# Counting a graph's edges on one core: ten blocks of 125 by 125 in a tile instead of five of 125 by 250, with the edge columns kept in two copies so that TensorE reads at fixed addresses

## The chip, the cores and the metric

The kernel runs as one program on one core of a Trainium2 chip. The time is the device time of one execution in microseconds. Before the change three runs took 710.77, 713.29 and 714.03 us; their median, 713.29 us, is the number that the changed kernel is set against.

## What is computed

A graph of 1250 nodes with 21250 edges, sorted by destination, goes through two graph-attention layers (eight heads of 128, then one of 768) and a feed-forward part with routed class tokens; each part starts with a layer norm and adds to its input. The attention of the reference is a softmax over the edges of each destination:

```python
e = jax.nn.leaky_relu(a_src[src] + a_dst[dst], NEG_SLOPE)
m = jax.ops.segment_max(e, dst, num_segments=n)
ex = jnp.exp(e - m[dst])
denom = jax.ops.segment_sum(ex, dst, num_segments=n)
alpha = ex / (denom[dst] + EPS)
out = jax.ops.segment_sum(alpha[:, :, None] * h[src], dst, num_segments=n)
```

The kernel makes the attention dense. It counts how often each pair (destination, source) occurs, takes the logarithm of the counts, and adds it to a 1250 by 1250 table of logits. What the change touches is how these counts are made.

## The kernel before

**Stages.** The first stage (0 to about 153 us) does three things side by side: it normalizes x and multiplies it by W1 in three parts (high by high, high by low, low by high; `products`, line L1336), it counts the edges (`count_edges` on TensorE, `one_hots` on VectorE), and it forms the attention vectors' products. Then come the eight heads (to about 405 us), the second layer's features, its attention, and the feed-forward part. The order on each engine is written out by hand.

**Counting.** The nodes are cut into NT = 10 tiles of NP = 125 destinations. A count matrix of one tile is 125 x 1250 and is stored as 125 rows by 1250 columns of another meaning: block w of SUB = 5 holds 25 destinations, its 125 rows are pairs (destination, group of 250 sources), and its GW = 250 columns are the source within its group. The edges lie in 170 chunks of CE = 125, one edge per partition. For a chunk and a block, VectorE compares the chunk's row number with an iota (`hotk`, 125 values) and its column number with an iota (`hotr`, 250 values); TensorE multiplies the two one-hot matrices, and so adds every edge of the chunk to the count in PSUM.

**Visits.** Since the edges are sorted, a block's edges lie in few neighbouring chunks. A small plan, made on VectorE from the first and last chunk of each block, gives each tile a first chunk (`start`), each block an offset (`away`), and the number of trips of a loop; with this input it is one trip for each of the ten tiles. A visit takes VISIT = 5 chunks. Chunks are kept in pairs for VectorE's sake, so `one_hots` builds TRIP = 3 pairs, six chunks, starting at an even one, and TensorE uses five of them: four at fixed places and a fifth that is the first or the last of the six, by the parity of the start. That fifth matmul reads at an address computed in registers (`end_of`, L1253); the four others are at L1251. L1242 and L1256 are small matmuls that open and close the sums.

**Who waits for whom.** Block w's one-hots are one buffer: VectorE waits for `hot_used[w]` before it writes it, TensorE for `hot_ready[w]` before it reads it. When a tile's counts are complete, ScalarE takes the logarithm, VectorE mends it (`mend`, L1949), and SyncE stores it and loads it back in the right shape. On VectorE the work between the one-hots of two tiles stands in this order: the next tile's row numbers (`local_rows`, L1913), the next tile's plan words loaded into registers (`plan_of`, L1917 and L1918), then `rows_of`, `column_scaled`, `rows_lower` (L1987) and `mend`. After tile 0 the attention vectors (`attz`, L2030), the low parts of W1 (L2038) and `wrow` (L2042) come instead. TensorE needs `attz` for L1387, `wrow` for L1393, and `rows_out` of tile t - 2 for `turn(t)` (L1266).

Of the kernel before, what the change touches and what calls it, by code (L numbers as in the profile page):

```python
# [41 lines left out]
SUB = 5  # L42
NW = NT * SUB
WD = N // NW
TRIP = 3
VISIT = 2 * TRIP - 1
NTRIP = (NCH + VISIT - 1) // VISIT
COLS = 2 * NCH + 4
# [44 lines left out]
def ds(start, size):  # L93
    return bass.ds(start, size)
# [65 lines left out]
def gnn_ffn_kernel(nc, x, src_cols, dst_cols, dst_rows, W1, W1T, as1T, ad1T, b1c, W2, W2T, as2T, ad2T,  # L160
# [8 lines left out]
    with ctx:  # L169
# [21 lines left out]
        plan = sb("plan", [1, 2 * NT], I32)  # L191
# [43 lines left out]
        pad0 = sb("pad0", [NP, 6 * N], F32, early)  # L235
# [17 lines left out]
        vm = sb("vm", [2 * NW, 1], F32, early)  # L253
        sixteens = sb("sixteens", [1, SUB], F32, early)
        nf = sb("nf", [1, NT, SUB], F32, early)
        st = sb("st", [1, NT], F32, early)
        off = [sb(f"off{i}", [1, NT, SUB], F32, early) for i in range(2)]
        sw = sb("sw", [1, NT, SUB], F32, early)
        need = [sb(f"need{i}", [1, NT, SUB], F32, early) for i in range(4)]
        offw = sb("offw", [1, NT, SUB], F32, early)  # L260
        trip = sb("trip", [1, NT], F32, early)
        trip2 = sb("trip2", [1, NT], F32, early)
        run = [sb(f"run{i}", [1, 20], F32, early) for i in range(5)]
        packed = sb("packed", [1, 2 * NT], F32, early)
# [6 lines left out]
        gcol = sb("gcol", [CE, COLS], F32, p1)  # L271
        r16 = sb("r16", [CE, COLS], F16, p1)
        g16 = [sb(f"g16_{p}", [CE, COLS], F16, p1) for p in range(2)]
        hotk = [sb(f"hotk{w}", [CE, TRIP, NP, 2], F16, p1) for w in range(SUB)]
        hotr = [sb(f"hotr{w}", [CE, TRIP, GW, 2], F16, p1) for w in range(SUB)]
        LCw = [sb("LCw0", [NP, SUB * GW], F32, p1)]
# [6 lines left out]
        LCw.append(sb("LCw1", [NP, SUB * GW], F32, p1))  # L283
# [14 lines left out]
        xT_first = sb("xT_first", [128, KD, NP], F32, p1)  # L298
        h1st = [sb(f"h1st{p}", [NP, HC], F32, p1) for p in range(2)]
# [112 lines left out]
        plan_step, g16_set = sem("plan_step"), sem("g16_set")  # L412
        hot_ready = [sem(f"hot_ready{w}") for w in range(SUB)]
        hot_used = [sem(f"hot_used{w}") for w in range(SUB)]
# [267 lines left out]
        def _(pool):  # L682
# [6 lines left out]
            pool.iota(tlo[:, :], pattern=[[WD, NW]], base=0, channel_multiplier=0,  # L689
# [5 lines left out]
            for w in range(SUB):  # L695
                pool.memset(sixteens[:, w:w + 1], float(16 ** w)).then_inc(consts_made, 1)
# [97 lines left out]
        def _(act):  # L794
# [34 lines left out]
            def log_counts(t):  # L829
                act.wait_ge(cnt_full, t + 1)  # L830
                freed(act, lc_stored[t % 2], TWO * (t // 2))
                for b in range(3):
                    c0, c1 = b * 2 * GW, min((b + 1) * 2 * GW, SUB * GW)
                    last = act.activation(LCw[t % 2][:, c0:c1], bank[b][0:NP, 0:c1 - c0], ACT.Ln,
                                          bias=tiny[:, 0:1], scale=2.0)
# [372 lines left out]
        def _(pe):  # L1208
# [6 lines left out]
            def spans_turned():  # L1215
# [3 lines left out]
                pe.transpose(bank[2][0:2 * NW, 0:NS], vv[:, :], ident[0:NS, 0:NS]).then_inc(span_turned, 1)  # L1219
                keep_busy(8)  # L1220
                pe.wait_ge(span_step, 7)
                pe.transpose(bank[2][0:1, 128:128 + 2 * NW], vm[:, :], ident[0:2 * NW, 0:2 * NW]
                             ).then_inc(span_turned, 1)

            def end_of(hot, odd):
                return hot[:, ds(2 * odd, 1), :, ds(odd, 1)].rearrange("p q n j -> p (q n j)")

            def count_plan(t):
                aways = pe.value_load(plan[0:1, t:t + 1], min_val=0, max_val=(1 << 4 * SUB) - 1)
                trips = pe.value_load(plan[0:1, NT + t:NT + t + 1], min_val=1, max_val=(NCH << 15) - 1)  # L1230
                start = (trips >> 15).with_bounds(min_val=0, max_val=NCH - 1)
                count = (trips & 63).with_bounds(min_val=1, max_val=NTRIP)
                before = ((trips >> 6) & 511).with_bounds(min_val=0, max_val=NT * NTRIP)
                return aways, start, count, before

            def count_edges(t, plan_of_t):
                aways, start, count, before = plan_of_t
# [578 lines left out]
        def _(dve):  # L1816
# [11 lines left out]

            dve.memset(attz[:, :, :], 0.0).then_inc(attz_set, 1)

# [25 lines left out]
            dve.tensor_reduce(vm[:, :], bank[2][0:2 * NW, 0:NS], mybir.AxisListType.X, ALU.max).then_inc(span_step, 1)  # L1856
# [5 lines left out]
            dve.tensor_scalar(qa[:, :], srcf[:, :], 1.0 / GW, 0.5 / GW - 0.5, ALU.mult, ALU.add).then_inc(edge_step, 1)  # L1862
# [4 lines left out]
            dve.memset(gcol[:, NCH:COLS], -1.0)  # L1867
# [638 lines left out]
```

## Time and profile before

| | |
|---|---|
| median of three runs | 713.29 us |
| the profiled execution's own time | 711.5 us |
| its span, first to last instruction | 709.7 us |
| TensorE busy | 698.6 us (98%) |
| VectorE busy | 528.8 us (75%) |
| ScalarE busy | 439.1 us (62%) |
| mean granted TensorE clock | 0.999 |

Engine names in the rows: PE is TensorE, PEld its weight loads, DVE VectorE, ACT ScalarE, SP SyncE. A letter q behind a name (DVEq, SPq) marks what the engine's instruction stream does itself: register arithmetic, loads of registers, branches, issues of transfers. Such records are not counted as busy time, and one such record holds up every instruction behind it until it is done. Times in the rows are us from the span's start, durations after a slash or marked as mean are ns. A busy TensorE need not be at its peak, since matmuls overlap.

### The profile page before, as it was taken

How to read it: one execution, taken by the hardware profiler on the slowest of the kernel's cores; microseconds unless marked ns; L12 is line 12 of the kernel's file. 1: busy time of each engine (PE TensorE's matmuls, PEld its weight loads, DVE VectorE, ACT ScalarE, POOL GpSimd, SP SyncE). 2: the span in 40 equal slices, each digit the busy share in tenths (PEclk: the TensorE clock that was granted, in tenths of full speed). 3: DMA queues.
4: the chain of work that ended last, by engine and by line, in shares of the span. 5: the costliest groups of instructions: out<-in, count | busy, mean ns of one | idle time of the engine just before them, and what ended most of it. 6: DMA issues, size and time to landing. Idle time of an engine off the chain costs nothing.

```text
span 709.7 us, 13757 instructions
## 1 busy us (share of the span) xinstructions
PE 698.6 (98%) x4705; PEld 655.6 (92%) x4705; DVE 528.8 (75%) x864; ACT 439.1 (62%) x898; POOL 146.9 (21%) x136
## 2 busy tenths in 40 slices
PE   8899999999999999999999999999999999999997
PEld 6699999888999999999999999999999899999997
DVE  5999888698999999999999664445568752737232
ACT  4665584387999999999999754553453333522202
POOL 2558121000112112121221000000223331323202
PEclk9999999999999999999999999999999999999999
DMA  8627887658633433443411431101882634315102
GB/s 285 215 69 199 255 249 218 183 148 247 199 71 76 94 69 84 81 99 59 92 21 21 123 116 59 59 0 37 253 276 64 207 92 189 102 57 178 44 23 66
DMA packets 48178, 88.35 MB, mean 124 GB/s; under 512 B 5263, under 2 KB 30831, under 8 KB 48128
## 3 DMA queue, kind: packets, MB, share of 16 engines
q1 hardware_dynamic: 37548, 65.69, 31.3%
q0 software_dynamic: 6080, 8.17, 7.4%
q10 hardware_dynamic: 4500, 13.82, 5.9%
q8 instruction: 31, 0.51, 0.3%
q14 instruction: 19, 0.16, 0.1%
HBM read 68.09 MB, written 15.33 MB: 118 GB/s over the span
## 4 chain that ended last, share of the span: by engine, by line
PE 90%; DVE 4%; DMA 4%; ACT 1%; issue 1%; POOL 0%; ACTq 0%; SPq 0%; DVEq 0%
PE bank L1479 19%; PE bank L1619 13%; PE bank L1440 12%; PE bank L1543 12%; PE bank L1336 11%; PE bank L1723 4%; DMA w1n_sb<-in_W 3%; PE bank L1695 3%; PE bank L1251 3%; PE bank L1597 2%; PE bank L1749 1%; DVE x2f L2359 1%; PE bank L1486 1%; PE bank L1485 1%; ACT w_hi L1035 1%; PE bank L1253 1%
## 5 line engine op out<-in xcount | busy, mean ns | idle before, releaser
L1479 PE MATMUL bank<-PT,h1s 125*128 125x250 f32 x660 | 147.5, 374 | 0.0
L1479 PEld LDWEIGHTS bank<-PT,h1s 125*128 125x128 f32 x660 | 121.2, 190 | 13.6
L2124 DVE SCALAR_TENSOR_TENSOR L<-asb,nad 125x1250 f32<-125x1250 f32 x80 | 121.3, 1551 | 2.5 <-DMA asb<-src_logit_rows 1.7
L2135 DVE CUSTOM_DVE_ANT_0 L<-L,LC 125x1250 f32<-125x1250 f32 x80 | 113.7, 1452 | 1.3
L950 ACT ACTIVATE L<-L,nm 125x1250 f32<-125x1250 f32 x80 | 109.7, 1373 | 7.1 <-DVE nm L2135 5.8
L1440 PE MATMUL bank<-ident,L 125*125 125x125 f32 x800 | 94.0, 273 | 0.0
L1440 PEld LDWEIGHTS bank<-ident,L 125*125 125x125 f32 x800 | 91.1, 189 | 0.8 <-issue 0.4
L971 ACT COPY PT<-bank 125x500 f32<-125x500 f32 x165 | 83.8, 616 | 1.9 <-PE bank L1440 1.9
L767 POOL DMA_DIRECT2D PT_diff<-PT x34 | 28.4, 836 | 157.9 <-ACT PT L971 157.9
L1932 DVE TENSOR_TENSOR hotr<-iota,r 125x1500 f16<-125x1500 f16 x50 | 46.6, 932 | 8.1 <-PE bank L1253 4.5
L1619 PE MATMUL bank<-h_hi,PT_hi 125*125 125x384 f32 x200 | 41.5, 350 | 0.0
L735 POOL TENSOR_TENSOR x<-x,b_sb 125x768 f32<-125x768 f32 x10 | 19.8, 1978 | 101.9 <-DMA fc2b_sb<-in_fc2b 92.6
L1619 PE MATMUL bank<-h_lo,PT_hi 125*125 125x384 f32 x200 | 40.4, 342 | 0.0
L1092 ACT ACTIVATE L<-L,nm 125x1250 f32<-125x1250 f32 x10 | 13.4, 1340 | 42.3 <-DVE nm L2279 42.3
L1619 PE MATMUL bank<-h_hi,PT_lo 125*125 125x384 f32 x200 | 38.1, 336 | 0.0
L1619 PEld LDWEIGHTS bank<-h_hi,PT_hi 125*125 125x125 f32 x200 | 34.0, 185 | 2.5 <-ACT PT_hi L1100 0.7
L2211 DVE COPY as2c<-bank 125x1 f32<-125x1 f32 x10 | 1.6, 158 | 45.6 <-ACT h_hi L1055 45.6
L1619 PEld LDWEIGHTS bank<-h_hi,PT_lo 125*125 125x125 f32 x200 | 35.1, 185 | 0.0
L1619 PEld LDWEIGHTS bank<-h_lo,PT_hi 125*125 125x125 f32 x200 | 34.9, 186 | 0.0
L1042 ACT ACTIVATE hT<-hT,b_sb x64 | 19.5, 387 | 24.6 <-DVE hT L2186 24.6
L2336 DVE TENSOR_TENSOR x2f<-bank,x2f 125x384 f32<-125x384 f32 x20 | 10.2, 551 | 29.6 <-PE bank L1723 27.9
L1543 PE MATMUL bank<-w_hi,h1Tt_hi 128*125 128x384 f32 (+1 forms) x160 | 31.1, 344 | 0.6 <-ACT w_hi L1035 0.5
(288 smaller groups left out, 1419.9 us busy)
## 6 DMA issues: line engine op xcount, KB each, us to landing
asb<-src_logit_rows SPq DMA_DIRECT2D x14, 416.5 KB, 3.5
atom_w<-in_atom_inT SPq DMA_DIRECT2D x5, 1152.0 KB, 12.6
atom_w<-in_atom_outT SPq DMA_DIRECT2D x5, 1152.0 KB, 9.7
log_count_scratch<-LCw SPq DMA_DIRECT2D x10, 546.9 KB
LC<-log_count_scratch SPq DMA_DIRECT2D x10, 546.9 KB
LCt<-log_count_scratch SPq DMA_DIRECT2D x10, 546.9 KB
h_scratch<-h1st ACTq DMA_DIRECT2D x10, 448.0 KB
PT_diff<-PT POOLq DMA_DIRECT2D x34, 122.1 KB, 3.0
```

What stands on the lines that cost most here:

```text
L767: pool.dma_start(PT_diff[p][:, :].bitcast(F32), PT[p][:, PART + 1, :], accum_op=ALU.add).then_inc(lower_moved[p], 16)
L950: e = act.activation(L[r][:, :], L[r][:, :], ACT.Exp, bias=nm[q][:, t:t + 1], scale=-1.0, accum_out=den[q][:, t:t + 1])
L971: act.copy(PT[(k - lag) % 2][:, 2 * b:2 * b + 2, :], turned[0:NP, 0:2 * GW].rearrange("p (s n) -> p s n", s=2)).then_inc(tb_evac, 1)
L1336: mm = pe.matmul(bank[b][0:NP, 0:c1 - c0], rows[t % 2][:, k, :], weights[:, k, c0:c1], start=(part == 0 and k == 0), stop=(part == 2 and k ...
L1440: mm = pe.transpose(bank[turned_bank(first, k - lag, b)][0:NP, (2 * s + j) * NP:(2 * s + j + 1) * NP], L[(2 * (k - lag) + j) % RING][:, (2 ...
L1479: mm = pe.matmul(sums, h1s[q][:, s, :], PT[p][:, s, :], start=(s == (0 if plain else PART + 2)), stop=(plain and s == NT - 1))
L1543: mm = pe.matmul(bank[2 * p + b][0:NP, 0:w], rows[p][:, k, :], weights[:, k, c0:c0 + w], start=(part == 0 and k == 0), stop=(part == 2 and ...
L1619: mm = pe.matmul(bank[2 + 2 * j + b][0:NP, 0:HALF], rows[:, s, j * NP:(j + 1) * NP], features[:, s, b * HALF:(b + 1) * HALF], start=(term ...
L1723: mm = pe.matmul(bank[down_bank(i, j) + b][0:NP, 0:HALF], rows[:, m, j * NP:(j + 1) * NP], weights[:, m, b * HALF:(b + 1) * HALF], start=( ...
L1932: dve.tensor_tensor(hotr[w][:, :, :, :], iota2[:, 0:GW, :].unsqueeze(1).to_broadcast([CE, TRIP, GW, 2]), r16[:, ds(2 * pair, 2 * TRIP)].re ...
L2124: dve.scalar_tensor_tensor(L[s % RING][:, :], asb[q][0:NP, 1, :], nad1[:, ds(h, 1), t:t + 1].rearrange("p h t -> p (h t)"), asb[q][0:NP, 0 ...
L2135: dve.tensor_tensor_reduce(out=L[s % RING][:, :], in0=L[s % RING][:, :], in1=LC[:, t, :], scale=-1.0, scalar=-FLOOR, op0=ALU.add, op1=ALU.min,
```

## The change

Each tile is counted in SUB = 10 blocks of 125 rows (12 or 13 destinations by 10 groups of 125 sources) and 125 columns. A visit takes three chunks, and two pairs of one-hots (TRIP = 2) are built for it. The row and column numbers are kept in two copies, the second shifted by one chunk, so that a visit that starts at an odd chunk starts at the first place of a pair in the other copy; TensorE then always uses the first three of the four chunks, at fixed addresses. With this input every block's edges still lie within one visit, so each tile is again one trip. The semaphores `hot_ready` and `hot_used` count blocks by twos. The plan has twice as many first chunks and offset words: VectorE loads four words for a tile in place of two, TensorE one in place of two. Row and column numbers are both 125 wide now, so the two one-hots of a block have the same size, and the store of the counts writes runs of 125 numbers in place of 250. Cut to its core:

```diff
-SUB = 5
+SUB = 10
+HW = SUB // 2
-WD = N // NW
-TRIP = 3
+WD = 13
+TRIP = 2
@@ TensorE
             def count_plan(t):
-                aways = pe.value_load(plan[0:1, t:t + 1], min_val=0, max_val=(1 << 4 * SUB) - 1)
-                trips = pe.value_load(plan[0:1, NT + t:NT + t + 1], min_val=1, max_val=(NCH << 15) - 1)
+                trips = pe.value_load(plan[0:1, 2 * (NT + t):2 * (NT + t) + 1], min_val=1, max_val=(NCH << 16) - 1)
...
-                    for w in range(SUB):
-                        out = bank[w // 2][0:NP, (w % 2) * GW:(w % 2 + 1) * GW]
-                        odd = ((start + (aways >> (4 * w)) + c) & 1).with_bounds(min_val=0, max_val=1)
-                        pe.wait_ge(hot_ready[w], before + c + 1)
-                        for q, j in ((0, 1), (1, 0), (1, 1), (2, 0)):
-                            pe.matmul(out, hotk[w][:, q, :, j], hotr[w][:, q, :, j], start=False, stop=True,
-                                      skip_group_check=True)
-                        mm = pe.matmul(out, end_of(hotk[w], odd), end_of(hotr[w], odd), start=False, stop=True,
-                                       skip_group_check=True)
-                        mm.then_inc(hot_used[w], 1)
+                    for v in range(HW):
+                        pe.wait_ge(hot_ready[v], before + c + 1)
+                        for w in (2 * v, 2 * v + 1):
+                            out = bank[w // 4][0:NP, (w % 4) * NP:(w % 4 + 1) * NP]
+                            for q, j in ((0, 0), (0, 1), (1, 0)):
+                                mm = pe.matmul(out, hot[w][:, 1, q, :, j], hot[w][:, 0, q, :, j], start=False, stop=True,
+                                               skip_group_check=True)
+                        mm.then_inc(hot_used[v], 1)
@@ VectorE, once
+            for p in range(2):
+                dve.memset(rg16[p][:, :, :, :], -1.0).then_inc(pads_set, 1)
...
+            for p in range(2):
+                dve.tensor_copy(pairs_of(p, 0), rcol[:, :, :].rearrange("p c (i j) -> p c i j", j=2)).then_inc(edge_step, 1)
@@ VectorE, one_hots
-                    for w in range(SUB):
-                        away = ((aways >> (4 * w)) & 15).with_bounds(min_val=0, max_val=15)
-                        pair = ((start + away + VISIT * c) >> 1).with_bounds(min_val=0, max_val=COLS // 2 - TRIP)
-                        dve.wait_ge(hot_used[w], before + c + 1)
-                        dve.tensor_tensor(hotr[w][:, :, :, :],
...
+                    for v in range(HW):
+                        dve.wait_ge(hot_used[v], before + c + 1)
+                        for w in (2 * v, 2 * v + 1):
+                            start, away = trips[w // HW] >> 16, (aways[w // HW] >> (4 * (w % HW))) & 15
+                            after = start + away + VISIT * c + 1
+                            pair = ((after >> 1) + (after & 1) * SPAN).with_bounds(min_val=0, max_val=PAIRS - TRIP)
+                            dve.tensor_tensor(hot[w][:, 0, :, :, :],
...
```

On VectorE, in the loop of `one_hots`, one block before the change reads as follows; REGISTER_ALU and ISA are register work of the instruction stream, an ISA row being a bundle of several operations (FUSED_REGOPS in the profile).

```order
L1932 REGISTER_ALU x2
L1932 ISA
L1932 TENSOR_TENSOR hotr<-iota,r 125x1500
L1936 REGISTER_ALU
L1936 TENSOR_TENSOR hotk<-iota,g_0 125x750
```

There are five of these in a tile. The same place of the changed kernel, one block of ten:

```order
L1959 REGISTER_ALU x2
L1959 ISA
L1959 REGISTER_ALU
L1959 ISA
L1959 TENSOR_TENSOR hot<-iota,rg_0 125x500
L1963 ISA
L1963 TENSOR_TENSOR hot<-iota,rg_0 125x500
```

A block of half the count matrix has the same number of vector instructions, smaller ones, and three bundles where there was one.

Behind the last block of tile 0, VectorE's stream before the change goes on with these rows; `plan` is the plan words, `g_1` the next tile's row numbers, `w_lo` the low parts of W1.

```order
L1913 TENSOR_SCALAR g_1<-gcol 125x344
L1917 TENSOR_LOAD plan
L1917 ISA x2
L1918 TENSOR_LOAD plan
L1918 ISA x2
L2030 COPY attz<-att 128x8 x2
L2038 TENSOR_TENSOR w_lo<-w_sb,w_hi 128x1024 x6
L2042 COPY wrow<-bank 16x192 x4
```

And after it:

```order
L1936 TENSOR_SCALAR rg_1<-gcol 125x2x172
L1941 TENSOR_LOAD plan
L1941 ISA x2
L1941 TENSOR_LOAD plan
L1941 ISA x2
L1943 TENSOR_LOAD plan
L1943 ISA x2
L1943 TENSOR_LOAD plan
L1943 ISA x2
L2058 COPY attz<-att 128x8 x2
L2066 TENSOR_TENSOR w_lo<-w_sb,w_hi 128x1024 x6
L2070 COPY wrow<-bank 16x192 x4
```

Two more loads, each with its bundle and its check of bounds, stand between the one-hots and `attz`; the same four loads stand at this place in every tile but the last.

On TensorE, the first two visits of a tile before the change:

```order
L1251 MATMUL bank<-hotr,hotk 125x250 x4
L1253 ISA
L1253 REGISTER_ALU
L1253 ISA x2
L1253 MATMUL bank<-hotr,hotk 125x250
```

After it, all visits of a tile with the loop's frame:

```order
L1248 MATMUL bank<-iota,zeros 125x16 x3
L1251 UNCONDITIONAL_BRANCH
L1251 ISA
L1253 REGISTER_ALU
L1253 ISA
L1257 MATMUL bank<-hot 125x125 x30
L1251 REGISTER_ALU x2
L1251 COMPARE_AND_BRANCH
L1260 MATMUL bank<-iota,zeros 125x16
```

Twenty-five matmuls of 250 columns with register work between them became thirty of 125 columns with none.

## Rows read from the trace of the kernel before

**Rows 1.** The page: the span, and VectorE's busy tenths in 40 slices.

```profile
span 709.7 us, 13757 instructions
DVE  5999888698999999999999664445568752737232
```

**Rows 2.** Windows, two tile periods: length; busy PE, PEld, DVE, ACT, POOL; clock; DMA; GB/s.

```profile
46.77:56.17 9.40, 9.40 (x70) 9.33 (x69) 9.40 (x17) 5.28 (x12) 9.40 (x1) 1.00 0.52 159
96.78:107.68 10.90, 10.81 (x81) 10.49 (x80) 9.64 (x17) 8.96 (x21) 3.30 (x5) 1.00 0.86 254
```

**Rows 3.** The chain that ended last, 0 to 60 us: start, us, what.

```profile
5.39 23.21 DMA w1n_sb<-in_W
...
28.65 2.79 PE bank L1387 x64
...
42.96 0.13 PE bank L1242 x3
43.09 0.50 PE bank L1251 x4
43.59 0.11 PE bank L1253
```

**Rows 4.** TensorE in order of time: start, us, instructions; tiles 1, 4 and 9.

```profile
42.80 0.29 PE L1242 MATMUL bank<-iota,zeros 125*125 125x16 f16 x3
...
45.83 0.84 PE L1266 MATMUL bank<-ident,xn 125*128 125x125 f32 x6
...
74.10 0.29 PE L1242 MATMUL bank<-iota,zeros 125*125 125x16 f16 x3
...
77.97 1.19 PE L1336 MATMUL bank<-w_hi,xT_hi 128*125 128x336 f32 x6
...
127.26 0.29 PE L1242 MATMUL bank<-iota,zeros 125*125 125x16 f16 x3
...
130.37 1.46 PE L1277 MATMUL bank<-xT,watt 128*16 128x125 f32 x12
```

**Rows 5.** VectorE in order of time, tiles 1, 5 and 9.

```profile
37.36 0.94 DVE L1932 TENSOR_TENSOR hotr<-iota,r 125x1500 f16<-125x1500 f16 x1 [0.51 <-issue]
38.22 0.54 DVE L1936 TENSOR_TENSOR hotk<-iota,g 125x750 f16<-125x750 f16 x1
38.68 0.93 DVE L1932 TENSOR_TENSOR hotr<-iota,r 125x1500 f16<-125x1500 f16 x1
...
75.73 0.94 DVE L1932 TENSOR_TENSOR hotr<-iota,r 125x1500 f16<-125x1500 f16 x1 [1.77 <-PE bank L1253]
...
124.88 0.55 DVE L1936 TENSOR_TENSOR hotk<-iota,g 125x750 f16<-125x750 f16 x1
```

**Rows 6.** Register work of single lines: ns min/median/max, first and last start.

```profile
L1932 DVEq FUSED_REGOPS  x4: 109/113/117, 37.7 to 39.1; - x4
L1932 DVEq FUSED_REGOPS  x50: 107/117/285, 16.8 to 120.9; - x50
L1917 DVEq TENSOR_LOAD <-plan x1: 314/314/314, 39.6 to 39.6; - x1
L1918 DVEq SEQ_ASSERT  x1: 23/23/23, 40.9 to 40.9; - x1
L1931 DVEq FUSED_REGOPS  x10: 51/51/58, 16.5 to 117.8; - x10
L2215 DVEq FUSED_REGOPS  x12: 69/72/81, 435.7 to 478.9; - x12
```

**Rows 7.** VectorE and TensorE in order of time between tiles 0 and 1.

```profile
23.93 0.24 DVE L2030 COPY attz<-att 128x8 f32<-128x8 f32 x2
24.08 6.89 DVE L2038 TENSOR_TENSOR w_lo<-w_sb,w_hi 128x1024 fp32r<-128x1024 f32 x6
31.51 1.45 DVE L2042 COPY wrow<-bank 16x192 f32<-16x192 f32 x4 [0.54 <-PE bank L1387]
...
33.53 0.54 PE L1393 MATMUL bank<-ident,wrow 16*128 16x16 f32 x6
```

**Rows 8.** Waits of SyncE's queue, 20 to 165 us: total, times, longest.

```profile
SPq L469 <- DVE LCw L1949: 62.3, 7, 22.6
```

More of the change, by code:

```diff
@@ L190, in gnn_ffn_kernel @@
         as1c = sb("as1c", [NP, 2])
-        plan = sb("plan", [1, 2 * NT], I32)
+        plan = sb("plan", [1, 4 * NT], I32)
         w_ctx = ExitStack()
@@ L252, in gnn_ffn_kernel @@
         vv = sb("vv", [NS, 2 * NW], F32, early)
[L253 to L260, printed above, removed]
+        vm = sb("vm", [NW, 2], F32, early)
+        sixteens = sb("sixteens", [1, HW], F32, early)
+        nf = sb("nf", [1, 2 * NT, HW], F32, early)
+        st = sb("st", [1, 2 * NT], F32, early)
+        off = [sb(f"off{i}", [1, 2 * NT, HW], F32, early) for i in range(2)]
+        sw = sb("sw", [1, 2 * NT, HW], F32, early)
+        need = [sb(f"need{i}", [1, 2 * NT, HW], F32, early) for i in range(4)]
+        offw = sb("offw", [1, 2 * NT, HW], F32, early)
         trip = sb("trip", [1, NT], F32, early)
-        trip2 = sb("trip2", [1, NT], F32, early)
+        trip2 = sb("trip2", [1, NT, 2], F32, early)
         run = [sb(f"run{i}", [1, 20], F32, early) for i in range(5)]
-        packed = sb("packed", [1, 2 * NT], F32, early)
+        packed = sb("packed", [1, 4 * NT], F32, early)
+        rcol = sb("rcol", [CE, 2, SPAN], F32, early)
+        gcol = sb("gcol", [CE, 2, SPAN], F32, early)
         early.close()
@@ L270, in gnn_ffn_kernel @@
         iota2 = sb("iota2", [CE, SUB * NP, 2], F16, p1)
[L271 to L276, printed above, removed]
+        pad_hot = sb("pad_hot", [CE, 160], F32, p1)
+        rg16 = [None, sb("rg16_1", [CE, 2, PAIRS, 2], F16, p1)]
+        hot = [sb(f"hot{w}", [CE, 2, TRIP, NP, 2], F16, p1) for w in range(SUB)]
+        LCw = [sb("LCw0", [NP, N], F32, p1)]
         xin = [sb("xin0", [NP, D], F32, p1)]
@@ L694, in _ @@
                       allow_small_or_imprecise_dtypes=True).then_inc(consts_made, 1)
-            for w in range(SUB):
+            for w in range(HW):
                 pool.memset(sixteens[:, w:w + 1], float(16 ** w)).then_inc(consts_made, 1)
@@ L1897, in _ @@
             then(dve.tensor_scalar(flat(need[3]), flat(need[2]), -1.5 * 2.0 ** 23, 1.0, ALU.add, ALU.max))
-            then(dve.tensor_reduce(run[0][:, 9:19], need[3][:, :, :], mybir.AxisListType.X, ALU.max))
+            then(dve.tensor_reduce(run[0][:, 9:19], flat(need[3]).rearrange("a (t w) -> a t w", t=NT), mybir.AxisListType.X, ALU.max))
             for i, shift in enumerate((1, 2, 4, 8)):
@@ L1918, in plan_of @@
-                trips = dve.value_load(plan[0:1, NT + t:NT + t + 1], min_val=1, max_val=(NCH << 15) - 1)
+                aways = [dve.value_load(plan[0:1, 2 * t + e:2 * t + e + 1], min_val=0, max_val=(1 << 4 * HW) - 1)
+                         for e in range(2)]
+                trips = [dve.value_load(plan[0:1, 2 * (NT + t) + e:2 * (NT + t) + e + 1], min_val=1, max_val=(NCH << 16) - 1)
+                         for e in range(2)]
                 return aways, trips
             def one_hots(t, aways, trips):
-                start = (trips >> 15).with_bounds(min_val=0, max_val=NCH - 1)
```

108 lines of the change are left out of this document (63 added, 45 removed).

## The prediction

> **What bounds the kernel now.** I read the page first. VectorE is at nine tenths or more in most slices up to a third of the span, and only there [rows 1]; the counting lies in the first 130 us, so I looked at that stretch by tiles. From one tile's first one-hot to the next's takes 9.40 us early on, with both engines busy for all of it, and 10.90 us later, where TensorE is still full and VectorE has 1.3 us to spare [rows 2]. So VectorE starts out as the bound, and TensorE takes over from tile 4 on: there VectorE waits for the buffers that TensorE holds (1.77 us ahead of tile 5) [rows 5]. The chain that ended last says the same of the start: a transfer of W1 until 28.65 us, and after it TensorE alone, the counting among it [rows 3]. The reader is to see that in this stage neither engine has much room: what is taken from one is worth no more than the other's slack, about 1 us a tile.
>
> **TensorE's part.** A tile's counting takes 3.03 us (42.80 to 45.83) where TensorE's stream is ahead, and 3.87 us (74.10 to 77.97) where it waits for the register work of the fifth matmul [rows 4]. I take 3.2 us as the mean of tiles 1 to 9. A matmul of 250 columns advances the chain by 0.11 to 0.125 us, one of 16 columns by 0.043 us [rows 3]; 125 columns lie between, and half of 250 is 0.06 us. Thirty of them and the four small ones are 2.05 us. So TensorE is relieved by 1.15 us a tile, 10 us over nine tiles (bounds: at 0.043 us 15 us, at 0.11 us nothing). Tile 0 ends before the W1 transfer does and gives nothing.
>
> **VectorE's engine.** The starts of hotr, hotk and hotr are 0.86 and 0.46 us apart for 1500 and 750 elements [rows 5]: 0.52 us per 1000 elements and 0.07 us fixed. An instruction of 500 is then 0.33 us. Ten were 5 x 1.31 = 6.55 us a tile; twenty are 6.6 us. The smaller count matrix of a visit brings VectorE nothing, since twice as many instructions and the unused fourth chunk eat it up. Its other work in a tile, 9.40 - 6.55 = 2.85 us [rows 2], stays.
>
> **VectorE's instruction stream.** Here the change costs. Before, the four bundles from 37.7 to 39.1 us are three blocks apart: 0.47 us of stream for a block whose vector work lasts 1.31 us [rows 6]. The stream runs ahead, and so the two plan loads, from 39.6 to 40.9 us, 1.28 us with their checks [rows 6], lie under one-hots that run until 44 us. After, a block has three bundles for one. A bundle of two operations (L1931) takes 51 ns, one of four (L2215) 72, the six-operation one of L1932 113 [rows 6]. The new ones hold four, five and three operations: about 82, 95 and 65 ns, by a line through these. With 35 ns between records a block becomes 0.47 - 0.11 + 0.24 + 2 x 0.035 = 0.67 us; I take 0.66, just the engine's 2 x 0.33. The stream no longer gains on the engine, so the four loads, 2.6 us, come into the open: `rows_of`, `rows_lower` and `mend` stand behind them. A tile of stream is then: 0.4 to enter the loop, 6.6 for ten blocks, 0.4 to leave it, 2.6 for the loads, 0.3 to hand over the rest: 10.3 us. The engine itself needs 6.6 + 2.85 = 9.45, TensorE 9 to 9.5. VectorE's stream sets the pace at 10.3 us where tiles 1 to 9 came at 10.2 on average (from 37.36 to the last hotk at 124.88, less the 4 x 1.31 + 0.86 = 6.1 that this one stands behind its tile's first, over 8) [rows 5]. TensorE's gain is thus not cashed, and two of its `turn`s wait some 2 us for `rows_of`, which are now behind the loads, inside this same pace.
>
> The bounds of a block: if all three bundles cost what the two-operation one does, 0.57 us, and the engine sets 9.5 us a tile; if each cost what the dearest of L1932 does, 285 ns (the first of a tile, with seven operations [rows 6]), 1.3 us and 16 us a tile. I take the near end, since no new bundle has more than five operations.
>
> **The start.** Between 4 and 14 us the plan is made in a row of small vector instructions. They get twice the elements (0.05 us each for about 20), two copies of row and column numbers, two casts: +1.6 us together by the 0.2 to 0.3 us that such instructions take. The four fills of pads fit into the idle time before the edges land. Two more loads add 1.3 us. So tile 0's one-hots start 2.9 us later and end at about 26.7. The stream leaves them at 26.4, loads until 29.1, and `attz`, done at 24.17 before, is done at 29.5. TensorE's L1387 was waiting for W1 until 28.65 [rows 3]; it loses 0.9. But VectorE then has 6.89 us for w_lo before `wrow`, which began at 31.51 after a wait of 0.54 [rows 7]. Now w_lo ends at 36.3, `wrow` at 37.7, and L1393 starts at 37.9 in place of 33.53 [rows 7]: +4.3 us on both engines up to tile 1's one-hots, at 41.7 in place of 37.36.
>
> **The sum.** Before, tile 9's counting ended at 130.37 and was TensorE's, 5 us after its one-hots [rows 4, 5]. After: the loop of tile 1 is entered at 40.9; eight paces of 10.3 give 123.3 for tile 9; its one-hots wait 1.6 us for `mend` and run 6.6, to 131.5; TensorE follows pair by pair and ends 0.4 later, at 131.9. What is behind is TensorE's as before. So +1.5 us: the late start costs 4.3, VectorE's lower pace takes what TensorE gains, and the 5 us by which TensorE lagged behind the last one-hots are what pays for it. The profiled execution took 711.5, its span is 709.7 [rows 1]; it would be 713.0, and the median of the runs, 1.8 higher, becomes 714.8.
>
> **The stores.** Runs of 250 numbers become runs of 125, 500 bytes. No row prices this; if a store took twice as long, SyncE's queue, which waits 62 us for `mend` in this stretch [rows 8], would take it, so the sum has 0. The Trainium skill, in DMA: Bandwidth & Descriptors, its table of rules at the top, gives 512 bytes as the least run for full rate and says that less is read, changed and written back; no run here shows it yet. By that page the stores get dearer than twice, and the rival below is the place where it would matter.
>
> **The rivals.**
> - *Even or nearly* (0.43): as summed. Its own range, with the block between 0.63 and 0.70 us, is 712 to 718.
> - *Faster* (0.20): the register work stays under the vector work. It decides at a block below 0.6 us or at loads that take under half of 2.6 us in the open. Then a tile costs 9.5: 8 x 0.8 = 6.4 less, minus 1 where TensorE's own work is then the limit: 1.5 - 5.4 = -3.9, 709.4. For it: the gap between records is my estimate, and L1932's bundle contains a division that may be its dear part. Against it: the count of the records.
> - *Slower, by the stream* (0.22): the bundle with a multiplication by 172 or the loads cost more; at 0.76 us a block a tile is 11.3, +8: 722.8. It decides from 0.70 us on. For it: a bundle of seven operations takes 285 ns where six take 113; nothing shows where the step is. Register loads were seen at 314 ns and they need not be quicker with the engine idle.
> - *Slower, by the clock* (0.10): the granted clock is 1.00 in these stretches, 2.4 GHz [rows 2]. TensorE would now stand idle twice, about 2 us before L1387 and 3 us before L1393, with thin work before. If the clock falls to 1.2 GHz there, the 3 us of matmuls up to tile 1's one-hots take 6: +3, 717.8. The Trainium skill, in TensorE: Matmul & The Clock Gate, says that an idle TensorE is held at the lower clock until it has been busy; by that page this rival is open, and the trace has no idle time of this length to decide it.
> - *Slower, by the stores* (0.05): if stores take 5 us more and the last ones hold up the loads that head 0 needs, +3: 717.8. Against it: [rows 8].
>
> **How the numbers follow.** Forecast 714.8. The faster case reaches to 709.4, the dearer stream to 722.8; 709 to 721.5 leaves out about 1 in 10 on either side. About 0.5%, 3.6 us, is what a measurement of this kernel tells from none. Faster by more than that: 0.20; within it: the even case less its upper edge, and small parts of the others, 0.44; slower: 0.36.
>
> **What would show it.** Right: one-hot instructions of 0.33 us from start to start; a gap of VectorE of about 0.8 us ahead of `rows_of` in each tile, put down to issue; L1393 at about 38 us; TensorE's counting of a tile stretched to the one-hots' pace, with waits for hot; the first one-hots of two tiles 10.3 us apart; VectorE's waits for TensorE gone. Wrong: FUSED_REGOPS of the new lines at 150 ns or more or below 60; loads under 0.2 us; `attz` before 28 us; a granted clock below 1 between 25 and 45 us; TensorE without waits in the counting, which would mean that its relief counts after all.

## The result: 1.6% slower, and the profile after

The changed kernel takes 723.8 us (four runs, 723.3 to 724.7). The kernel before, timed beside it, takes 712.3. The ratio is 1.0164, 95% interval 1.0144 to 1.0184. The profiled execution has a span of 721.5 us where [rows 1] have 709.7.

The page of the changed kernel: span, VectorE's 40 slices, TensorE's granted clock in the same slices, and the chain that ended last by engine and by line.

```profile
span 721.5 us, 14196 instructions
...
DVE  7778788889989999999999684444568762737332
...
PEclk9899999999999999999999999999999999999999
...
PE 75%; DVE 11%; DVEq 8%; issue 5%; ACT 1%; POOL 0%; ACTq 0%
PE bank L1483 18%; PE bank L1623 13%; PE bank L1444 12%; PE bank L1547 11%; DVEq L1959 4%; PE bank L1727 4%; PE bank L1699 3%; PE bank L1340 3%; DVE hot L1963 2%; DVE hot L1959 2%; PE bank L1601 2%; DVEq L1943 1%; DVEq L1941 1%; PE bank L1753 1%; DVE x2f L2387 1%
```

DVEq is VectorE's sequencer, its instruction stream. With L1959 (the addresses) and L1941 and L1943 (the plan words) it stands on the chain that decides. VectorE's and TensorE's order of time, as in [rows 4, 5], tiles 1 to 3 and 9:

```profile
42.72 0.42 DVE L1959 TENSOR_TENSOR hot<-iota,rg 125x500 f16<-125x500 f16 x1 [0.74 <-issue]
...
43.43 0.42 DVE L1959 TENSOR_TENSOR hot<-iota,rg 125x500 f16<-125x500 f16 x1
...
49.84 0.33 DVE L1936 TENSOR_SCALAR rg<-gcol 125x344 f16<-125x344 f32 x1
52.12 0.28 DVE L1994 COPY rows<-bank 8x125 f32<-8x125 f32 x1 [1.95 <-issue]
...
54.74 0.40 DVE L1959 TENSOR_TENSOR hot<-iota,rg 125x500 f16<-125x500 f16 x1
61.33 0.32 DVE L1936 TENSOR_SCALAR rg<-gcol 125x344 f16<-125x344 f32 x1
63.85 0.28 DVE L1994 COPY rows<-bank 8x125 f32<-8x125 f32 x1 [2.21 <-issue]
...
66.47 0.40 DVE L1959 TENSOR_TENSOR hot<-iota,rg 125x500 f16<-125x500 f16 x1
...
132.98 0.40 DVE L1959 TENSOR_TENSOR hot<-iota,rg 125x500 f16<-125x500 f16 x1
```

```profile
49.51 0.29 PE L1248 MATMUL bank<-iota,zeros 125*125 125x16 f16 x3
...
60.34 2.04 PE L1257 MATMUL bank<-hot 125*125 125x125 f16 x30
...
140.60 2.59 PE L1281 MATMUL bank<-xT,watt 128*16 128x125 f32 x12
```

The first one-hots of two tiles are 12.02 and 11.73 us apart early on. From tile 1 (42.72) to tile 9 (132.98) the mean is 90.26 / 8 = 11.3 us, where 10.2 stood before and 10.3 was forecast. TensorE's thirty matmuls do take 2.04 us where they are not held up, as forecast. Yet the count of tile 9 ends at 140.60 in place of 130.37 [rows 4]: 10.2 us later. The start carries 5.4 of them (42.72 for 37.36 [rows 5]), eight paces 8.8, tile 9's own one-hots 0.3, and TensorE's lag behind the last one-hots, 4.9 us before and 0.6 now, gives 4.3 back. What follows starts 11.8 us late, and this is the loss of the span.

Between tiles 0 and 1, TensorE's order of time, to hold against [rows 7]:

```profile
30.39 4.99 PE L1391 MATMUL bank<-w1n_sb,attz 128*16 128x192 f32 x64 [1.81 <-DVE attz L2058]
35.32 2.21 PE L1340 MATMUL bank<-w_hi,xT_hi 128*125 128x352 f32 x12
38.49 0.54 PE L1397 MATMUL bank<-ident,wrow 16*128 16x16 f32 x6 [0.97 <-DVE wrow L2070]
```

L1397 (L1393 before) starts at 38.49 for a forecast of 37.9. L1391 took 4.99 us where the same 64 matmuls took 2.79 [rows 3]; the granted clock of 28 to 32 us was 0.51, so this is the 1.2 GHz level. It was granted before the wait of 1.81 us began, while TensorE was kept waiting by tile 0's one-hots. Windows of that stretch: length; busy PE, PEld, DVE, ACT, POOL; clock; DMA; GB/s.

```profile
26.00:28.00 2.00, 0.75 (x8) 0.61 (x9) 2.00 (x7) 1.49 (x4) 0.00 (x0) 1.00 0.58 137
28.10:28.50 0.40, 0.40 (x7) 0.38 (x4) 0.00 (x0) 0.40 (x2) 0.00 (x0) 0.50 0.22 85
```

The register work of a tile, whole kernel: nanoseconds min/median/max, first and last start.

```profile
L1959 DVEq ALU_OP  x300: 40/45/50, 19.9 to 139.0; - x150
L1959 DVEq FUSED_REGOPS  x200: 93/151/234, 20.0 to 139.0; - x100
L1963 DVEq FUSED_REGOPS  x100: 64/64/71, 20.6 to 139.2; - x100
L1941 DVEq TENSOR_LOAD <-plan x20: 299/306/1350, 16.7 to 129.4; - x20
```

A block has six records: three single operations of 45 ns (three a block as before) and three bundles. The second bundle, the one that multiplies by 172, takes 151 ns. In tile 1, where VectorE follows its stream, a block takes (49.84 - 42.72) / 10 = 0.71 us. In tile 2 the one-hots come 0.66 us apart (54.74 to 61.33 for ten), at the engine's own pace. The stream works them out from 52.6 on, under `mend`; it has this lead of 2 us, loses part of it at 0.71 us a block, and the loads use up the rest. So the sum of the stream is what sets the pace. Two more views of it: the loop entries of tiles 1 to 9 (MOVE, one a tile), and the single operations of tile 2.

```profile
L1952 DVEq MOVE  x9: 36/36/43, 41.6 to 131.3; - x9
...
L1959 DVEq ALU_OP  x30: 40/45/47, 52.6 to 59.9; - x30
```

The entries are (131.3 - 41.6) / 8 = 11.2 us apart, and in between the stream never stands for more than 0.45 us. Tile 1's 10.7 us are 0.4 to enter the loop, 7.3 for ten blocks (the first takes 0.87), 0.3 to leave it, 2.5 for the loads and 0.2 to go on. The other tiles have 0.6 us more on average: half is one pause of 0.40 to 0.45 us in six of them, half is loads that last up to 1.35 us (L1941 above). What causes these two, no run shows.

### The profile page after: what moved, and what is told of

It is laid out like the page before. It is cut to its first block, busy times and chain, and to the rows that moved or that the text cites. A ratio compares the mean times of both kernels' runs of the same rounds, so it can differ in the third digit from the quotient of the medians.

```text
span 721.5 us, 14196 instructions
## 1 busy us (share of the span) xinstructions
PE 698.5 (97%) x4757; PEld 654.2 (91%) x4757; DVE 535.6 (74%) x968; ACT 438.6 (61%) x898; POOL 139.0 (19%) x136
## 4 chain that ended last, share of the span: by engine, by line
PE 75%; DVE 11%; DVEq 8%; issue 5%; ACT 1%; POOL 0%; ACTq 0%
PE bank L1483 18%; PE bank L1623 13%; PE bank L1444 12%; PE bank L1547 11%; DVEq L1959 4%; PE bank L1727 4%; PE bank L1699 3%; PE bank L1340 3%; DVE hot L1963 2%; DVE hot L1959 2%; PE bank L1601 2%; DVEq L1943 1%; DVEq L1941 1%; PE bank L1753 1%; DVE x2f L2387 1%
## 5 line engine op out<-in xcount | busy, mean ns | idle before, releaser
L1959 DVE TENSOR_TENSOR hot<-iota,rg 125x500 f16<-125x500 f16 x100 | 40.7, 407 | 4.8 <-issue 4.7
L1963 DVE TENSOR_TENSOR hot<-iota,rg 125x500 f16<-125x500 f16 x100 | 40.5, 405 | 0.0
L714 POOL TENSOR_SCALAR var<-mv 125x1 f32<-125x1 f32 x9 | 20.6, 2289 | 84.1 <-ACT xin L890 80.3
```

The source lines that it names most:

```text
L1959: dve.tensor_tensor(hot[w][:, 0, :, :, :], iota2[:, 0:NP, :].unsqueeze(1).to_broadcast([CE, TRIP, NP, 2]), rg16[t % 2][:, 0, ds(pair, TRIP ...
L1963: made = dve.tensor_tensor(hot[w][:, 1, :, :, :], iota2[:, w * NP:(w + 1) * NP, :].unsqueeze(1) .to_broadcast([CE, TRIP, NP, 2]), rg16[t % ...
```

## The experiments

Theory 1: VectorE's instruction stream (register work and plan loads) is what costs. Theory 2: the clock that TensorE is granted after idle time. Theory 3: the shorter runs of the stores. Two more came up on the way.

**Fixed addresses.** The first chunk of each block is a constant.

```diff
-    start, away = trips[w // HW] >> 16, (aways[w // HW] >> (4 * (w % HW))) & 15
-    after = start + away + VISIT * c + 1
-    pair = ((after >> 1) + (after & 1) * SPAN)
+    after = CHUNKS[t][w] + 1
+    pair = after // 2 + after % 2 * SPAN
```

> The changed kernel with the first chunk of each block written into VectorE's instructions as a constant for this input (VectorE loads no plan words and works out no addresses; the plan is still made, and TensorE still reads its own part of it). Theory 1, VectorE's instruction stream (four loads in the open and three bundles of register operations a block) sets the pace: the one-hots come at 0.33 us each, a tile falls from about 11.7 us to 9.5, eight tiles give 17 us, the start another 3, and TensorE takes some of it back as the next bound: 702 to 709 us, below the kernel before (712). Theory 2, the loss is TensorE's own (a lower clock, idle time that it makes itself): the count of tile 9 moves by under 4 us, 719 to 724. Theory 3, the shorter runs of the stores: nothing changes by more than 1 us, 723 to 725.

Measured: 713.2 us, ratio 1.0032 (1.0015 to 1.0049). That is 10.6 below the changed kernel, but none of the theories has this number. VectorE's order of time shows a tile of 9.44 us, which is the 6.6 + 2.85 of the prediction, and TensorE's and GpSimd's show what came in its place:

```profile
40.42 0.41 DVE L1965 TENSOR_TENSOR hot<-iota,rg 125x500 f16<-125x500 f16 x1
...
49.85 0.40 DVE L1965 TENSOR_TENSOR hot<-iota,rg 125x500 f16<-125x500 f16 x1
...
59.29 0.40 DVE L1965 TENSOR_TENSOR hot<-iota,rg 125x500 f16<-125x500 f16 x1
```

```profile
46.53 0.85 POOL L724 TENSOR_SCALAR var<-mv 125x1 f32<-125x1 f32 x1 [11.32 <-ACT xin L900]
47.46 19.14 POOL L726 TENSOR_TENSOR rstd<-var,powers 125x1 f32<-125x1 f32 x1
66.59 17.45 POOL L724 TENSOR_SCALAR var<-mv 125x1 f32<-125x1 f32 x1
84.12 9.79 POOL L726 TENSOR_TENSOR rstd<-var,powers 125x1 f32<-125x1 f32 x1
```

```profile
94.02 1.42 ACT L869 ACTIVATE h1st<-bank,rstd 125x352 f32<-125x352 f32 x3 [8.96 <-POOL rstd L726]
...
94.72 5.49 PE L1350 MATMUL bank<-w_hi,xT_hi 128*125 128x352 f32 x18 [8.03 <-ACT h1st L869]
```

VectorE now works without a gap from 40.4 to 93.5 us, and GpSimd's instructions on one number a partition, 0.19 and 0.55 us where VectorE stands, last 10 to 19 us. `rstd` is late, ScalarE can't scale, TensorE stands 8.03 us and then runs its 18 matmuls in 5.49 us for 3.10, at the lower clock (0.51 granted from 94.7 to 100.2). GpSimd (POOL in the rows) got in at 93.9, when VectorE had stopped, and at 66.6 and 84.1, while VectorE ran `rows_of`, whose two instructions read PSUM; at 47.4 and 57.1 `rows_of` passed and it did not. Call this theory P: GpSimd isn't served under unbroken one-hots.

**Loads later.** The next tile's plan words are loaded behind `rows_of`, `mend` and `rows_lower`, tile 1's behind `w_lo`.

```diff
-                    return plan_of(t + 1)
...
-            ahead = one_hots(2, *ahead)
+            one_hots(2, *plan_of(2))
```

> The changed kernel with the four loads of the next tile's plan words issued behind the tile's other work (rows_of, mend, rows_lower) in place of ahead of it, and those of tile 1 behind w_lo. Theory 1a, what costs is that the loads stand in the open while TensorE waits for what is behind them: attz comes 2.5 us earlier, tile 1's first one-hot at about 39 us in place of 42.7, and in each tile the loads lie half under the last of the other work: 8 x 0.7 more: 713 to 716 us. Theory 1b, stream and engine time add up wherever the loads stand, since the stream gets no further ahead than an instruction or two: only the start is gained, 719 to 721 us. Theory 3, the stores: 723 to 725.

Measured: 722.9 us, ratio 1.0173 (1.0149 to 1.0196). `attz` came 2.1 us earlier (27.95) and the gap ahead of `rows_of` was gone, as theory 1a wanted, but the gap stood ahead of the one-hots instead (0.5 to 2.7 us, by issue). Where the loads stand doesn't matter; 1b holds in kind and was 2 to 4 us too hopeful in size. Of the 2.1 us at `attz`, which L1397 still had (36.40 for 38.49), 1.2 were lost between L1397 and tile 1 at TensorE's lower clock (0.51 from 38 to 45 us): tile 1's first one-hot came at 41.81, 0.9 us earlier and not 3.7.

**Interleaved copies.** Pair s holds chunks s and s + 1, so the address is the chunk's number. The loads stay.

```diff
-    return flat[:, 1:1 + 2 * (SPAN - 1)].rearrange("p (c s) -> p c s", c=2)[:, :, 0:NCH]
+    return flat[:, 1:1 + 2 * NCH].rearrange("p (s c) -> p s c", c=2)
...
-    after = start + away + VISIT * c + 1
-    pair = ((after >> 1) + (after & 1) * SPAN)
...
-    rg16[t % 2][:, 0, ds(pair, TRIP), :]
+    rg16[t % 2][:, 0, 1:PAIRS, :][:, ds(after, 4), :].rearrange("p (q e) j -> p q e j", e=2)[:, :, 0, :]
```

> The changed kernel with the two copies of the edge columns interleaved pair by pair (pair s holds chunks s and s+1), so that the address is the first chunk itself: two bundles of register operations a block (six or seven operations and three) in place of three, and no multiplication by 172. Theory 1, the stream: a block falls from 0.72 us to 0.56 to 0.60, the engine's 0.66 then bounds it, and a tile gives 0.6 us: 718 to 720 us. Theory 1b, the four loads alone are the cost and the bundles lie under the vector work: 722.5 to 724. Theory 2 and 3: no change, 723 to 725.

Measured: 719.1 us, ratio 1.0118 (1.0101 to 1.0135), within what theory 1 gave, but for another sum. The register work of a block, and where the loads of one tile stand:

```profile
L1958 DVEq ALU_OP  x200: 45/45/50, 19.9 to 131.0; - x100
L1958 DVEq FUSED_REGOPS  x100: 93/93/244, 20.0 to 131.1; - x100
...
L1941 DVEq TENSOR_LOAD <-plan x2: 302/302/302, 55.9 to 56.5; - x2
```

and VectorE in order of time:

```profile
52.02 0.40 DVE L1958 TENSOR_TENSOR hot<-iota,rg 125x500 f16<-125x500 f16 x1
58.61 0.32 DVE L1936 TENSOR_SCALAR rg<-gcol 125x344 f16<-125x344 f32 x1
58.85 0.27 DVE L1995 COPY rows<-bank 8x125 f32<-8x125 f32 x1
...
61.46 0.40 DVE L1958 TENSOR_TENSOR hot<-iota,rg 125x500 f16<-125x500 f16 x1
```

In tile 1 nine of L1958's bundles begin between 42.7 and 46.3 us: a block is 0.45 us of stream, 0.2 under the engine's 0.66. In tile 2 the first load starts at 55.9, 2.7 us ahead of L1936, and all four lie under one-hots. In the changed kernel a tile's first load starts 0.7 us ahead of L1936 (60.6 for 61.33). Tile 1's whole stream, loads and all, is now 8.4 us (loop entries at 41.2 and 49.6), less than the engine's 9.44, and from tile 2 on it is the stream that waits (0.5 to 1.2 us at each loop entry). So the blocks' register work, which I had put just at the engine's pace, decides whether 2.5 us of loads are seen. The gain was then lost at 115 us: `rstd` and `var` of tiles 7 and 8 were held from 96.3 to 115.3 us and TensorE stood 5.17 and 2.63 us. Theory P again.

**TensorE's relief alone,** in the kernel before.

```diff
-    pe.matmul(out, hotk[w][:, q, :, j], hotr[w][:, q, :, j], ...)
+    pe.matmul(out[:, 0:NP], hotk[w][:, q, :, j], hotr[w][:, q, 0:NP, j], ...)
```

> The kernel before with the first four of the five matmuls of a block cut to half of their columns, so that half of each count but for one chunk is left out: TensorE is relieved by about 20 x 0.055 = 1.1 us a tile, near what the change promises, and VectorE is left alone. Theory A, TensorE bounds the later tiles: five or six tiles give 1.1 us each, 706 to 708 us. Theory B, TensorE lags but VectorE sets the pace: 1 to 3 us at the end of tile 9, 709 to 712.

Measured: 711.3 us, ratio 0.999 (0.9973 to 1.0008), in the range of theory B. But the run doesn't decide between A and B, since TensorE was hardly relieved. TensorE in tile 7:

```profile
107.38 0.40 PE L1251 MATMUL bank<-hotr,hotk 125*125 125x125 f16 x4
...
107.99 0.40 PE L1251 MATMUL bank<-hotr,hotk 125*125 125x125 f16 x4
...
108.61 0.40 PE L1251 MATMUL bank<-hotr,hotk 125*125 125x125 f16 x4
```

Blocks are 0.61 us apart with half the columns, where whole ones were 0.56 apart in the kernel before (106.99, 107.55). The kernel before has 0.62 us a block in tile 4, with whole columns and the same register work. So I put this pace down to TensorE's own address work. Over tiles 1 to 9 the count takes 3.06 us a tile for 3.21, not 1.1 less. Columns alone bring TensorE little; with fixed addresses as well, thirty matmuls take 2.04 us.

**Is it GpSimd?** Three kernels leave GpSimd one instruction a tile in place of two or three: one on top of fixed addresses, one on top of the kernel before, one on top of the interleaved copies.

```diff
-    pool.tensor_scalar(var[p][:, :], mv[p][:, 1:2], 1.0 / D, LN_EPS, ALU.mult, ALU.add)
+    act.activation(var[p][:, :], mv[p][:, 1:2], ACT.Copy, bias=LN_EPS, scale=1.0 / D)
...
-    pool.tensor_scalar(nmr[p][:, :], stats[p][:, 0, 0:1], rstd[:, t:t + 1], None, ALU.mult)
+    act.activation(nmr[t % 2][:, :], stats[t % 2][:, 0, 0:1], ACT.Copy, scale=rstd[:, t:t + 1])
```

> The kernel with fixed addresses, and GpSimd left with one instruction a tile (the power of -0.5); the scaling of the sum and, for the last two tiles, nmr are ScalarE's. In the kernel with fixed addresses VectorE ran from 40.4 to 93.5 us without a gap, GpSimd's three instructions of 125x1 elements lasted from 47.46 to 93.9 us in place of about 2, and TensorE stood 8.03 us at 94.7. Theory P, GpSimd's small instructions only get in where VectorE stops, so fewer of them are held up for less: the 8 us and most of the clock's fall behind them are gone, 702 to 706 us. Theory Q, the stall is another's and GpSimd's spans only look long: 712 to 714 us.

Measured: 713.0 us, ratio 1.0025 (1.0005 to 1.0046). The kernel with fixed addresses had 713.2: nothing gained. GpSimd in order of time:

```profile
52.13 11.15 POOL L725 TENSOR_TENSOR rstd<-var,powers 125x1 f32<-125x1 f32 x1 [7.73 <-ACT var L893]
63.46 46.17 POOL L725 TENSOR_TENSOR rstd<-var,powers 125x1 f32<-125x1 f32 x4 [0.17 <-ACT var L893]
```

Four instructions in 46.17 us. The stall moved on to 111 us (TensorE 4.61 and 2.87 us). The number of instructions is not what costs. The part of theory P on which I had built the expectation was wrong; its first half, not served under unbroken one-hots, fits better than before.

> The kernel before, with GpSimd left with one instruction a tile in the same way. Its rstd of tile 3 lasted 19.08 us under VectorE's unbroken one-hots, but nothing waited for it. Theory P: no wait to remove, 710.5 to 713 us. Theory Q: the same. If GpSimd's delays did cost the kernel before something, below 709 us.

Measured: 712.1 us, ratio 1.001 (0.9992 to 1.0027). In the kernel before, GpSimd's delays cost nothing that can be measured.

> The kernel with interleaved copies, and GpSimd left with one instruction a tile. With interleaved copies a tile took 9.44 to 9.5 us of VectorE from tile 2 on, with all loads and register work hidden, until rstd and var of tiles 7 and 8, held from 95.2 to 115.4 us, made ScalarE's xn late and TensorE stand 5.17 and 2.63 us. Theory P: these 7.8 us are gone, less what TensorE then has to wait elsewhere, 710 to 713 us. Theory Q: 718 to 720 us.

Measured: 710.8 us, 707.5 to 718.3, ratio 0.998 (0.9939 to 1.0022). The median is where theory P had it, but the runs spread over 11 us, so this one is inconclusive. The trace, of the 718.3 us run, has the same stall as fixed addresses with one instruction: four instructions in 45.81 us, and TensorE stands 4.45 and 3.58 us.

**The clock.** 28 unused transposes in the idle time ahead of L1397, with interleaved copies.

```diff
+    keep_busy(28)
     pe.wait_ge(watt_done, 1)
```

> The kernel with interleaved copies, and 28 transposes of 128 columns whose result is not used, ahead of TensorE's transposes of wrow (L1397), where it stood 3.18 us and then ran at a granted clock of 0.50 for about 9 us. Theory 2, the clock: with TensorE busy there the clock stays at 1.00, the 10 us of matmuls from 36.65 to 47 us take 5 us less, 713 to 716 us, unless VectorE's own lateness holds tile 1. Rival, VectorE sets the time of tile 1 and after anyway: 718 to 720 us.

Measured: 718.4 us, ratio 1.0088 (1.0059 to 1.0117): in the rival's range, and 0.8 under the kernel without them, which is within the two intervals. The clock of 40 to 60 us was 1.00 where 0.85 stood, and ScalarE's first piece of tile 1 behind it began at 48.41 for 50.16. 1.75 us of start were gained where I expected 3 to 6. In this run L1391 came at the lower clock (4.28 us, 2.79 in the other), and TensorE waited 8.68 us up to 108.65 for ScalarE's `h1st`; ScalarE had waited 7.29 us for GpSimd's `var` (until 105.55). So the clock costs a little at the start, and the trace puts most of what is lost elsewhere.

**A pause for GpSimd.** Nothing is taken away; VectorE waits once a tile.

```diff
+    if t > 2:
+        dve.wait_ge(rstd_ready, 2 * t + 1)
     dve.wait_ge(g16_set, t + 1)
```

> The kernel with fixed addresses, with one wait more on VectorE ahead of the one-hots of tiles 3 to 9: until GpSimd's rstd of that tile is there. Nothing else changes; GpSimd keeps its three instructions. Theory P, GpSimd gets in only where VectorE stands, whatever the number of its instructions (one a tile was held as long as three): each wait costs VectorE 0.6 to 1.2 us, no GpSimd instruction lasts over 10 us, and the 8 us in which TensorE stood are gone: 703 to 709 us. Theory Q, the stall has another cause and the waits only add to it: 716 us or more.

Measured: 704.8 us, ratio 0.9913 (0.9881 to 0.9944): one wait more makes the kernel 8.4 us faster. VectorE and GpSimd around two of the waits:

```profile
57.58 0.42 DVE L1967 TENSOR_TENSOR hot<-iota,rg 125x500 f16<-125x500 f16 x1 [0.45 <-POOL rstd L726]
...
75.89 0.42 DVE L1967 TENSOR_TENSOR hot<-iota,rg 125x500 f16<-125x500 f16 x1 [0.45 <-POOL rstd L726]
```

```profile
45.23 12.32 POOL L726 TENSOR_TENSOR rstd<-var,powers 125x1 f32<-125x1 f32 x1
57.53 0.19 POOL L724 TENSOR_SCALAR var<-mv 125x1 f32<-125x1 f32 x1
57.80 0.61 POOL L726 TENSOR_TENSOR rstd<-var,powers 125x1 f32<-125x1 f32 x1
```

`rstd` is held for 12.32 us and ends as soon as VectorE stops. VectorE waits for it in four of the seven tiles, 0.45 us each, less than the 0.6 to 1.2 expected. TensorE's longest wait from then to 130 us is 1.70, and its count takes 2.0 to 2.1 us in every tile from 1 to 9: here its relief is cashed, and the kernel is 7 us faster than the kernel before. Three instructions of GpSimd still lasted over 10 us (12.32, 11.13 and 11.17), against the expectation, without harm. This decides for theory P against Q. That it is VectorE's way to SBUF which keeps GpSimd out is argued and not tested by itself.

> The kernel with interleaved copies, GpSimd with one instruction a tile, and VectorE waiting for it ahead of the one-hots of tiles 3 to 9. Theory P: 0.5 to 0.7 us a wait, 4 to 5 us in all, against 7.8 us of TensorE's idle time and its lower clock: a tile takes 10.0 us, tile 9's count ends near 130 us, and the time is 708 to 711 us. Theory Q: 718 to 722 us.

Measured: 708.9 us, ratio 0.9951 (0.9933 to 0.9969). The interleaved copies, the plan read at run time as in the changed kernel, one GpSimd instruction and the pause: 2.8 us faster than the kernel before. VectorE waited for GpSimd once, 1.26 us, where 4 to 5 us in all were expected; TensorE's longest wait in the later tiles was 1.92 us (102.37). Since two things were added to the interleaved copies, this run alone doesn't tell them apart.

> The kernel above, with the start changed too: wrow copied behind the third of the six pieces of w_lo (L1397 of TensorE waits for it), tile 1's plan words loaded behind w_lo, and 8 transposes that are not used ahead of L1397. Theory 2 with the late start: TensorE's idle time there falls from 3.2 us to under 1.5 in a piece, the clock stays at 1.00 for more of it, and tile 1's count starts at 46 to 47 us in place of 49.8: 704 to 708 us. Rival, VectorE's start of tile 1 decides and it moves by under 1 us: as the kernel above.

The start's edit, beside the loads of tile 1 behind `w_lo`:

```diff
     for k in range(KD):
         ...
+        if k == 2:
+            dve.wait_ge(wattp, 1)
+            for c in range(4):
+                r = dve.tensor_copy(wrow1[:, c * QW:(c + 1) * QW], bank[5][32 * c:32 * c + 2 * H, 0:QW])
```

Measured: 709.1 us, ratio 0.9965 (0.9949 to 0.9981). The forecast of 704 to 708 was missed. Tile 1's count began at 47.07 for 48.30 in the kernel above, and its first one-hot at 39.99 for 41.40; by the median nothing of it was left, and where it went was not followed. The wait for `wrow` was gone, 1.17 us came in its place for `w_lo` (ahead of L1378, which is L1374 in the changed kernel), and the clock of 40 to 44 us was 0.58.

**The stores,** in the kernel before.

```diff
-    flat.rearrange("(w p r) -> p w r", w=SUB, p=NP)
+    flat.rearrange("(w p r) -> p w r", w=2 * SUB, p=NP)
```

> The kernel before, with LCw stored in runs of 125 numbers, 500 bytes, in place of 250 (the same bytes, the numbers of each row at other places of the scratch tensor, so the log counts that come back are permuted). Theory 3, the stores cost: over 715 us. Theory 1 and 2, the stores lie hidden: 711 to 713 us, with over 17,000 packets under 512 bytes in place of 5,263.

Measured: 712.1 us, ratio 1.0005 (0.9992 to 1.0018). The page's count of packets:

```profile
DMA packets 54428, 88.35 MB, mean 125 GB/s; under 512 B 17763, under 2 KB 37081, under 8 KB 54378
```

12,500 more packets under 512 bytes, and no time that shows: by the interval it is at most 1.3 us. SyncE's queue waits 62.3 us for `mend` as in [rows 8].

## Why the prediction was wrong, point by point

**The direction of each step was right, the size of one decided.** The forecast was 714.8 with a range to 721.5; the time is 723.8. It fell to the rival "slower, by the stream" (722.8 at 0.76 us a block and 11.3 us a tile), which had 0.22: the tile is 11.3 us.

**The step that failed** is the cost of the stream, "a block becomes 0.67 us; I take 0.66", and with it the 6.6 us for ten blocks. The rows show 0.71 us for a block, 0.87 for the first, and 7.3 us for ten. One term was mis-sized: the second bundle was put at 95 ns by a line through bundles without such a multiplication; it takes 151. The bundles of four and three operations, forecast at 82 and 65 ns, took 95 and 64, so the three are 310 ns and not 242. Two terms were missing. The first bundles of a tile are dearer (234 and 167 ns), though [rows 6] had shown this for L1932 (285 for 117). And the pauses and long loads, 0.6 us a tile on average, were in no sum; their cause stays open.

**The rest of that sum held.** "VectorE's stream sets the pace" and the loads "come into the open": both are what the rows show. 0.4 us to enter, 0.3 to leave, 2.5 for the loads without the long ones and 0.2 to go on are 3.4 us, for 3.7 in the forecast. With 7.3 for ten blocks and 0.6 of pauses and long loads that is 11.3. The gap ahead of `rows_of` came to 1.4 to 2.5 us and not 0.8, because the gap is what the stream's pace has over the engine's 9.45. With interleaved copies, which take 0.26 us off a block, the stream's tile is 8.4 us, the gap is gone, and the tile is the engine's 9.44. So the loads are seen when the tile's whole stream is longer than the engine's tile. By these numbers (3.4 us beside ten blocks, against 9.45) that begins at a block of 0.6 us, my estimate, which is where the prediction put its faster rival.

**The start** was nearly right: the first one-hot of tile 0 came at 20.57 (20.0 by the sum, 2.9 after the 17.13 of before), `attz` began at 30.04 (29.5 was forecast for its end), w_lo took 6.90 us, L1397 began at 38.49 (37.9). By tile 1 it was 1 us late, 42.72 for 41.7.

**TensorE's part** was right in size, 2.05 us (60.20 to 62.25) as forecast, and in that it isn't cashed: its `turn`s wait 1.09 and 2.21 us for `rows_of`, and in all TensorE waits 7.9 us for one-hots. "The 5 us of lag pay for it" held: 4.3.

**The clock** had 0.10, as a rival of its own. It came beside the stream, not in place of it: 4.99 for 2.79 us at L1391, mostly hidden since L1397 then waited for `wrow`, and behind tile 9 L1281's work of 1.46 us takes 2.59, which is most of the 1.6 us by which the later stage (11.8) is later than the count (10.2). The prediction tied the fall to idle times of 2 and 3 us. The granted clock fell at 28.1 us, where TensorE had stood 0.86 us at most at a time, but twice. It fell again later (0.50 from 86.2 to 89.5, for one). The trace of before, at 1.00 throughout, could not show this.

**The faster rival** (0.20, 709.4) was sound as a mechanism: at a block under 0.6 us a tile was to cost 9.5, and with interleaved copies or fixed addresses it does, 9.44. But the price it was given left out a third engine. At 9.44 us VectorE has no gap, GpSimd isn't served, and the 8 us come back as a stall. [rows 1 to 8] show of GpSimd only its two busy columns, one of them 9.40 in a window of 9.40 for one instruction [rows 2]. That column was the hint, and I read past it. In the changed kernel TensorE never waits behind GpSimd from tile 0's count to the end of tile 9's count, so this didn't make it slow; it is why removing the stream's cost alone brings 10 us and not 19.

**The stores** (0.05): no cost that shows, in the kernel before. By the Trainium skill, DMA: Bandwidth & Descriptors, section Specifications, runs under 512 bytes get dearer; here they may, but the queue's wait for `mend`, unchanged at 62.3 us, leaves room for it.

## What to carry to other kernels

When an instruction's address is worked out at run time, add up the sequencer's records over a whole period of the loop, the loads and the dearer first bundle included, and hold the sum against the engine's time for the same period. Here 8.4 us against 9.44 hid four loads, and 11.2 showed them. Before an engine is made denser, look at which small instructions of another engine get in only where it stands, and whether anything waits for them: a planned pause of 0.45 us was worth 8 us.

## What the runs showed of the hardware

- GpSimd against VectorE. A GpSimd instruction on 125x1 numbers in SBUF takes 0.55 us when VectorE stands. Under back-to-back one-hots (two inputs in SBUF each) it lasts up to 19.14 us, and four of them 46.17 us. In the kernels with fixed addresses such an instruction ended within 0.5 us of VectorE's stop (93.91 for 93.50), or at times during the two PSUM reads of `rows_of`. GpSimd's spans in a profile are rough, but ScalarE's 8.96 us and TensorE's 8.03 us of waiting for it are not. The Trainium skill, in SBUF — State Buffer, "Who interferes with whom", says that a VectorE instruction with two SBUF inputs keeps out a GpSimd instruction that reads SBUF, until the first finishes. The trace agrees that it is kept out, and goes further: not until one instruction of 0.4 us finishes, but through a whole run of them. By the page's rule alone the delay would be about one instruction of VectorE, 0.4 us under one-hots: an estimate.
- Register work on VectorE's sequencer. A single operation 45 ns, a bundle of three 57 to 64, of four 95, of six with multiplications by 2 alone 93, of five with one by 172 151 ns; a plan word 0.30 us to load, at times up to 1.35, and 0.62 with its checks. The counts of operations are the program's. The time doesn't go by their number; that the multiplication by 172 makes the dear bundle is likely, and no run isolates it.
- TensorE's own address work. A block with 4 x 125 + 250 columns took 0.61 us and one with 5 x 250 took 0.62 us where the register work set the pace, and 0.56 us where it didn't. That the register work is the cause is read from these paces, not tested.
- TensorE's clock. The granted clock fell to 0.50 at 28.1 us in the changed kernel, after TensorE had been busy 0.75 us of the last 2, in short runs of matmuls with waits of 0.86 us between them. In the kernel before, a wait of 0.94 us did not bring it down (1.00 throughout).
